# One-tile expert units from the ninth last routing batch on, and expert weights laid out by partition

## The chip, the cores and the metric

The kernel runs on one core of a Trainium2 chip. The metric is the device time of one execution in microseconds (us), the median of three. A core has TensorE (PE, matrix products; PEld is its weight load), VectorE (DVE), ScalarE (ACT), GpSimd (POOL) and SyncE (SP), each with its own queue of instructions, and 16 DMA engines that move data between DRAM and on-chip memory. Engines meet only at semaphores: an instruction that waits holds up everything behind it on its engine.

## The reference

A graph layer for 12,500 nodes of 256 features and 212,500 edges, followed by a mixture of 8 experts:

```python
xn = _layernorm(x)
x = x + gnn(xn, src, dst, edge_weight, ...) + mix(xn, ...)
h = _layernorm(x)
# experts: D = 256, F = 1024, E = 8, C = ceil(1.25 * 12500 / 8)
idx = argmax(softmax(h @ gate_w + gate_b)); prb = its probability
pos = running count of tokens of the same expert; kept = pos < C
y = (relu(h @ w1[idx] + b1[idx]) @ w2[idx] + b2[idx]) * prb * kept
x = x + nan_to_num(y)
```

`gnn` gathers `xn[src]` for each edge, weights it and sums it by `dst`. All data are 32-bit floats.

## The kernel before

**Pairs.** The edges are cut into 416 groups of 512, taken two at a time: 208 pairs. The program of every engine runs over "places" `p`. In each place below `PAIRS` (208) POOL gathers the rows of a pair (8 indirect DMAs, L776, into a ring of three pairs), DVE builds the one-hot matrices, PE multiplies (L855) and turns the sums (L865), DVE adds them to `acc` (L1283).

**Tokens.** From place `FIRST_C` (57) on a tile `t` of 128 tokens enters as soon as its edges are summed (`enters`) and passes nine steps in the following places (`c_step`): mixing, graph output, normalisation, the gate's logits. The last of 98 tiles enters in place 207. Tiles are routed in 20 batches (`routes`): first of seven tiles, then of four, the last of three. Routing finds each token's expert and position and a table that lists, for each slot of 128 tokens, which tokens are in it. A batch is known at `slots_at`; the last at place 219 (`last_c`).

**Expert units.** A unit is a pair of slots of one expert, 256 tokens. `units_after(b)` is how many units are sure to be full after batch `b`, whatever the routing; the last batch brings all the rest. There are K = 56 units, 112 slots. A unit has five ticks. In tick 0 PE transposes its rows (L1014), in ticks 1 to 4 it does two of the eight 128-wide chunks of the first layer each (L1024); the second layer of a tick (L1043) follows one tick later. ACT copies the transposed rows (L1742), applies relu (L1751) and scales the result (L1758). DVE adds the bias (L1517) and cleans the result (L1523 to L1528) during the next unit.

**Planner.** Ticks are laid into places by a budget of PE time (`PE_PLACE`, `PE_EXPERT`, `PE_STEP`), at most two in one place up to `last_c` and one in each after it. From the tick places follow those of the loads by SP (`load_first` L649, L651 and `load_second` L658, L660, one expert's weights for each unit, two buffers), of the row gathers by POOL (`gather_unit` L792) and of the results: units that are done before place 207 are kept by SP in DRAM (`keep_unit` L665), loaded back four at a time (`load_back` L676) and added to `out` by POOL later, in quiet places (`scatter_back` L813); the others are added by POOL directly (`scatter_unit` L802). A result buffer (`yo`, three of them) is free once its unit is kept or added.

**Order on an engine.** In a place, POOL does: gather of the first group, unit gathers, gather of the second, scatters, back-scatters. PE does: the pair's products, then `early` (small routing products), unit ticks, `late` (token steps).

Of the kernel before, what the change touches and what calls it, by code (L numbers as in the profile page):

```python
# [29 lines left out]
def build(nc, x, src, dst, weight, dst_grouped, gnn_w1t, gnn_b1, gnn_w2t, gnn_b2,  # L30
          wqt_bq, wkv, bkv, v_gamma, v_beta, k_scale, mix_w1, mix_b1, mix_w2, mix_b2,
          gate_w, gate_b, ffn_w1, ffn_b1, ffn_w2, ffn_b2, out, edges):
# [7 lines left out]
    FF = ffn_w1.shape[2]  # L40
# [9 lines left out]
    EXPERT_UNITS = SLOT_TILES // UNIT_TILES  # L50
    K = (N + NE * (UNIT - 1)) // UNIT
    SLOTS = K * UNIT_TILES
    TICKS = 1 + FC // 2
# [7 lines left out]
    assert GJ * GROUP * P <= LAP and UNIT_TILES * H * P <= 512 and FC % 2 == 0  # L61
# [6 lines left out]
    with ctx:  # L68
# [19 lines left out]
        kept_d = nc.dram_tensor("kept_scratch", [-(-K // BACK_UNITS), P, BACK_ROWS * D], F32).ap()  # L88
# [151 lines left out]
        def early_row(c):  # L240
# [3 lines left out]
        w1_sb = [behind(0, H, FF) for _ in range(2)]  # L244
        w2_sb = [behind(0, FC, D) for _ in range(2)]
        b1_sb = [behind(0, FC) for _ in range(2)]
# [14 lines left out]
        (col_i, col_odd, col_tile, col_from, full_at, some_at, count, full, fresh, ranked, queue_at, queue_base) = (  # L261
            behind(1, 1) for _ in range(12))
# [154 lines left out]
        def units_after(b):  # L417
# [6 lines left out]
        batch_of = [next(b for b in range(len(routes)) if k < units_after(b)) for k in range(K)]  # L424

        def small_steps(p):
# [10 lines left out]
            for b in range(len(routes)):  # L437
                if slots_at[b] == p and units_after(b) > units_after(b - 1):
                    found.append(("slots", b))
# [11 lines left out]
        e_ticks = [(k, j) for k in range(K) for j in range(TICKS)] + [(K, j) for j in range(TICKS)]  # L451
# [31 lines left out]
        def place_of(k, j):  # L483
            return e_place[k * TICKS + j]


        w1_at, w2_at, gather_at, scatter_at = ([[] for _ in range(PLACES)] for _ in range(4))
        for k in range(K):
# [5 lines left out]
            lag = 3 if place_of(k + 1, TICKS - 1) < PAIRS - 3 else 1  # L494
            scatter_at[min(place_of(k + 1, TICKS - 1) + lag, PLACES - 1)].append(k)

        KEEP_BEFORE = PAIRS - 1
        kept = [k for p in range(KEEP_BEFORE) for k in scatter_at[p]]
        assert kept == list(range(len(kept)))
        keep_at = [scatter_at[p] if p < KEEP_BEFORE else [] for p in range(PLACES)]  # L500
        scatter_at = [[] if p < KEEP_BEFORE else scatter_at[p] for p in range(PLACES)]
# [15 lines left out]
        def y_value(k):  # L517
            return 16 * UNIT_TILES * sum(i >= len(kept) for i in range(k % YS, k + 1, YS))
# [37 lines left out]
        assert SLOT_AT + 3 * UNIT_TILES * max(units_after(b) - units_after(b - 1) for b in range(len(routes))) <= 2 * P  # L556

        def relu_value(k, j):
            return 2 * ((TICKS - 1) * k + j)

        def l1_value(k, j):
            return (TICKS - 1) * k + j


        def sync_program(sp):
# [75 lines left out]
            def expert_of(k):  # L641
                sp.wait_ge(q_ready, sum(units_after(b) > units_after(b - 1) for b in range(batch_of[k] + 1)))
                return sp.value_load(expert_i[:, UNIT_TILES * k:UNIT_TILES * k + 1], min_val=0, max_val=NE - 1)

            def load_first(k):
                x_ = expert_of(k)
                if k >= 2:
                    sp.wait_ge(l1_relu, relu_value(k - 2, TICKS - 1))
                sp.dma_start(w1_sb[k % 2], ffn_w1[bass.ds(x_, 1)].rearrange("a (h p) f -> p (a h) f", p=P)  # L649
                             ).then_inc(w1_ld[k % 2], 16)  # L650
# [1206 lines left out]
```

## Time and profile before

| | |
|---|---|
| Median of three runs | 2673.07 us (2669.90 to 2673.34) |
| Profiled execution | 2668.34 us, its span 2666.6 us |
| PE busy | 2188.9 us (82%) |
| POOL busy | 1921.0 us (72%) |
| DVE busy | 1468.1 us (55%) |
| ACT busy | 995.7 us (37%) |
| DRAM read, written | 444.96 MB, 74.40 MB |
| Mean granted TensorE clock | 0.94 |

Times in rows are microseconds from the start of the span. "Idle before" is the time for which the engine stood before the instruction, and what it waited for; "issue" means that it waited for nothing that the profile shows. PE records two matmuls for each product of 32-bit floats in the program, so L1024 and L1043 have 32 records each per two-tile unit. The clock is the share of full speed: 1.00 is 2.4 GHz and 0.50 is 1.2 GHz.

### The profile page before, as it was taken

The numbers are of one execution on the slowest core, as the hardware profiler recorded it, in microseconds if no ns is written. First come the engines' busy times: TensorE is split into PE (matmuls) and PEld (weight loads), VectorE is DVE, ScalarE is ACT, GpSimd is POOL, SyncE is SP. The second block draws the span as 40 slices with busy tenths as digits, with TensorE's granted clock in tenths as the row PEclk, the third lists the DMA queues.
The fourth block names the chain that finished last, engine by engine and source line by source line (L and its number), as shares of the span: only waits on it lengthen the run. The fifth ranks groups of instructions, "written<-read, shape, count | busy, mean of one in ns | idle before, by whom it ended". The sixth has DMA issues, their size and how long they took to land. (4 is left out here: it accounts for less than half of the span.)

```text
span 2666.6 us, 40750 instructions
## 1 busy us (share of the span) xinstructions
PE 2188.9 (82%) x12096; PEld 1675.1 (63%) x12096; DVE 1468.1 (55%) x4510; ACT 995.7 (37%) x2211; POOL 1921.0 (72%) x1905
## 2 busy tenths in 40 slices
PE   0079999995667887989989988889889998879997
PEld 0036555553455655777767766777777776768886
DVE  5855544444357776777646545655554555552222
ACT  4623222220244444554433433433334334323332
POOL 7267777777777777777777777777777777457772
PEclk9999999997799998999999999998999898979999
DMA  9655555554466667666677666666656666669973
GB/s 331 227 164 166 163 160 160 160 163 122 141 183 179 180 175 238 193 208 198 211 217 229 213 211 211 199 207 211 217 188 204 209 190 214 187 179 248 234 201 89
DMA packets 347352, 518.45 MB, mean 194 GB/s; under 512 B 59554, under 2 KB 266258, under 8 KB 346004
## 3 DMA queue, kind: packets, MB, share of 16 engines
q0 software_dynamic: 101376, 243.85, 33.3%
q1 hardware_dynamic: 215366, 233.56, 27.7%
q10 hardware_dynamic: 30390, 38.41, 4.0%
q8 instruction: 101, 1.65, 0.3%
q14 instruction: 119, 0.97, 0.1%
HBM read 444.96 MB, written 74.40 MB: 195 GB/s over the span
## 5 line engine op out<-in xcount | busy, mean ns | idle before, releaser
L776 POOL DMA_INDIRECT rows_sb<-xn_scratch,src_sb x1600 | 1564.5, 978 | 539.5 <-issue 533.7
L855 PE MATMUL bank<-rows_sb,s_sb 128*48 128x256 f32 x3200 | 436.0, 419 | 240.7 <-DMA rows_sb<-xn_scratch,src_sb 238.6
L855 PEld LDWEIGHTS bank<-rows_sb,s_sb 128*48 128x48 f32 x3200 | 224.8, 133 | 381.9 <-issue 267.0
L1043 PE MATMUL bank<-acc 128*128 128x256 f32 x1792 | 433.3, 386 | 9.5 <-DVE acc L1517 9.5
L1024 PE MATMUL bank<-acc 128*128 128x256 f32 x1792 | 433.3, 388 | 0.0
L1043 PEld LDWEIGHTS bank<-acc 128*128 128x128 f32 x1792 | 342.9, 194 | 56.9 <-issue 9.1
L1024 PEld LDWEIGHTS bank<-acc 128*128 128x128 f32 x1792 | 341.4, 195 | 44.2
L1283 DVE TENSOR_TENSOR acc<-acc,bank 128x96 f32 x416 | 106.1, 255 | 439.2 <-PE bank L865 193.1
L1751 ACT ACTIVATE acc<-bank,acc 128x256 f32<-128x256 f32 x448 | 188.0, 471 | 405.1 <-PE bank L1024 405.0
L1677 ACT COPY sums<-bank 112x256 f32<-112x256 f32 x208 | 76.8, 369 | 556.8 <-PE bank L855 556.7
L1708 ACT ACT_TABLE_LOAD x95 | 121.9, 1283 | 173.8 <-PE bank L946 172.9
L886 PE MATMUL bank<-arena 128*128 128x512 f32 x392 | 185.6, 596 | 0.0
L802 POOL DMA_INDIRECT out_dram<-acc,sca_i x48 | 75.2, 1566 | 101.7 <-DVE acc L1528 89.1
L792 POOL DMA_INDIRECT acc<-h_scratch,gat_i x112 | 110.7, 988 | 43.0 <-issue 30.5
L931 PE MATMUL bank<-arena,weff 128*128 128x128 f32 (+1 forms) x784 | 114.4, 292 | 28.8 <-ACT arena L1732 28.8
L931 PEld LDWEIGHTS bank<-arena,weff 128*128 128x128 f32 x784 | 106.9, 204 | 44.2 <-issue 41.0
L813 POOL DMA_INDIRECT out_dram<-rows_sb,sca_i x64 | 103.2, 1612 | 34.7 <-issue 18.6
L1267 DVE TENSOR_TENSOR s_sb<-s_sb,wgt_sb 128x384 f32<-128x384 f32 x208 | 116.8, 562 | 7.1
L1692 ACT ACTIVATE arena<-bank 128x512 f32<-128x512 f32 x98 | 58.5, 597 | 159.2 <-PE bank L886 159.2
L1361 DVE TENSOR_TENSOR arena<-bank,bias_sb 128x256 f32<-128x256 f32 x98 | 41.2, 420 | 135.1 <-PE bank L946 134.8
L1265 DVE TENSOR_TENSOR s_sb<-rel_sb,iota_win 128x384 f32<-128x384 f32 x208 | 113.7, 546 | 3.0 <-PE bank L855 1.6
L942 PE MATMUL bank<-w2m_sb,arena 128*128 128x256 f32 x392 | 107.8, 400 | 4.3 <-DVE arena L1366 4.3
(221 smaller groups left out, 3388.8 us busy)
## 6 DMA issues: line engine op xcount, KB each, us to landing
acc<-ffn_w_in SPq DMA_DIRECT2D x112, 1024.0 KB, 6.2
rows_sb<-xn_scratch,src_sb POOLq DMA_INDIRECT x1600
arena<-xn_scratch SPq DMA_DIRECT2D x194, 128.0 KB, 3.0
xnt_scratch<-arena SPq DMA_DIRECT2D x97, 128.0 KB
arena<-xnt_scratch SPq DMA_DIRECT2D x97, 128.0 KB
arena<-x_in SPq DMA_DIRECT2D x97, 128.0 KB
h_scratch<-arena ACTq DMA_DIRECT2D x97, 128.0 KB
out_dram<-arena ACTq DMA_DIRECT2D x97, 128.0 KB
```

Source lines behind the costliest of these rows:

```text
L776: pool.indirect_dma_start(out=rows_sb[:, c % ROW_SLOTS, :], out_offset=None, in_=xn_d, in_offset=bass.IndirectOffsetOnAxis(ap=src_sb[:, c: ...
L792: pool.indirect_dma_start(out=xs[:, k % 2 * UNIT_TILES + i, :], out_offset=None, in_=h2_d[0:tokens, :], in_offset=bass.IndirectOffsetOnAxi ...
L855: m = pe.matmul(psum[0][i * HALF:i * HALF + WIN, 0:D], s_sb[:, p % S_SLOTS, i * GROUP + j, :], early_row(c) if p < EARLY_PAIRS else rows_s ...
L886: m = pe.matmul(kv[0:r, :], xnt[:, t % R1, h, 0:r], wkv_sb[:, h, :], start=False, stop=h == H - 1)
L931: m = pe.matmul(psum[2][:, f * P:f * P + r], weff[:, h, f * P:(f + 1) * P], c_xnt[:, t % XS, h, 0:r], start=h == 0, stop=h == H - 1)
L942: pe.matmul(mix, c_hid[:, par, f, 0:r], w2m_sb[:, f, :], start=f == 0, stop=f == H - 1)
L1024: m = pe.matmul(bank[:, i * UNIT:(i + 1) * UNIT], w1_sb[k % 2][:, h, f * P:(f + 1) * P], xt[:, k % 2, h, :], start=h == 0, stop=h == H - 1)
L1043: m = pe.matmul(bank[:, i * D:(i + 1) * D], hid[:, f, i * P:(i + 1) * P], w2_sb[k % 2][:, f, :], start=f == 0 and i == 0, stop=f == FC - 1 ...
L1265: link(dve.tensor_tensor(s, rel_sb[:, c0:c0 + c].unsqueeze(2).broadcast_to(wide), iota_win[:, :].unsqueeze(1).broadcast_to(wide), ALU.is_e ...
L1267: dve.tensor_tensor(s, s, wgt_sb[:, c0:c0 + c].unsqueeze(2).broadcast_to(wide), ALU.mult).then_inc(s_built, 1)
L1708: act.activation(c_hid[:, par, f, 0:r], psum[2][:, f * P:f * P + r], ACT.Gelu, bias=beff[:, f:f + 1]).then_inc(c_gelu, 1)
L1751: act.activation(hid[:, f, :], bank[:, i * UNIT:(i + 1) * UNIT], ACT.Relu, bias=b1_sb[k % 2][:, f:f + 1]).then_inc(l1_relu, 1)
```

## The change

From the ninth last batch on (`SINGLE_FROM`) a unit is one slot of 128 tokens. There are then 105 slots in 82 units: 23 of two tiles and 59 of one. A one-tile unit has three ticks: the transposes, and two with four chunks of the first layer each. Cleaning a result is tied to the tick at which its unit ended (`last_tick`, `FLUSH`) instead of to the next unit's ticks. Only two-tile units are kept and loaded back (23; before 32). The quiet places of the back-scatters are chosen anew: up to two in one place, and one unit in each unit after the last token. The first-layer weights and its bias are one array, laid out so that a partition reads one run of 8,224 bytes; the second-layer weights likewise, 8,192 bytes. Before, a partition read two runs of 4,096 bytes and one of 32, and eight runs of 1,024.

```diff
-    K = (N + NE * (UNIT - 1)) // UNIT
-    SLOTS = K * UNIT_TILES
+    SLOTS = (N + NE * (P - 1)) // P
+    SINGLE_BATCHES = 9
+    FLUSH = 5
...
+        def tiles_after(b):
             if b < 0:
                 return 0
             if b == len(routes) - 1:
-                return K
-            return max(0, ((routes[b][-1] + 1) * P - NE * (UNIT - 1)) // UNIT)
+                return SLOTS
+            tokens = (routes[b][-1] + 1) * P
+            if b < SINGLE_FROM:
+                return UNIT_TILES * max(0, (tokens - NE * (UNIT - 1)) // UNIT)
+            return max(0, (tokens - NE * (P - 1)) // P)
+        units = []
+        for b in range(len(routes)):
+            size = UNIT_TILES if b < SINGLE_FROM else 1
+            units += [(b, at, size) for at in range(tiles_after(b - 1), tiles_after(b), size)]
...
+        def per_tick(k):
+            return 2 * UNIT_TILES // size(k)
+        def ticks(k):
+            return 1 + FC // per_tick(k) if k < K else FLUSH
+        def done_place(k):
+            return e_place[last_tick[k] + FLUSH]
...
-        kept = [k for p in range(KEEP_BEFORE) for k in scatter_at[p]]
+        kept = [k for p in range(PAIRS - 1) for k in scatter_at[p] if size(k) == UNIT_TILES]
...
-        quiet = [p for p in range(PAIRS + 2, last_c + 4) if not gather_at[p]]
-        for k in range(K):
-            if place_of(k, 0) > last_c + 4:
-                quiet += [place_of(k, 1), place_of(k, 3)][:1 + k % 2]
+        quiet = [p for p in range(PAIRS + 2, last_c + 4) if not gather_at[p] for _ in range(1 + (p > PAIRS + 3))]
+        quiet += [place_of(k, 1) for k in range(K) if place_of(k, 0) > last_c + 4]
...
-                sp.dma_start(w1_sb[k % 2], ffn_w1[bass.ds(x_, 1)].rearrange("a (h p) f -> p (a h) f", p=P)
-                             ).then_inc(w1_ld[k % 2], 16)
-                sp.dma_start(b1_sb[k % 2], ffn_b1[:, bass.ds(x_, 1), :].rearrange("p a c -> p (a c)")
+                sp.dma_start(first_sb[k % 2], ffn_first[bass.ds(x_, 1)].rearrange("a p f -> p (a f)")
                              ).then_inc(w1_ld[k % 2], 16)
...
-                sp.dma_start(w2_sb[k % 2], ffn_w2[bass.ds(x_, 1)].rearrange("a (c p) d -> p (a c) d", p=P)
+                sp.dma_start(flat2(w2_sb[k % 2]), ffn_w2[bass.ds(x_, 1)].rearrange("a p f -> p (a f)")
...
-                        for i in range(2):
-                            f = 2 * (j - 1) + i
+                        for i in range(per_tick(k)):
+                            f = per_tick(k) * (j - 1) + i
                             for h in range(H):
-                                m = pe.matmul(bank[:, i * UNIT:(i + 1) * UNIT], w1_sb[k % 2][:, h, f * P:(f + 1) * P],
-                                              xt[:, k % 2, h, :], start=h == 0, stop=h == H - 1)
+                                m = pe.matmul(bank[:, i * tokens:(i + 1) * tokens], w1_sb[k % 2][:, h, f * P:(f + 1) * P],
+                                              xt[:, k % 2, h, 0:tokens], start=h == 0, stop=h == H - 1)
...
+    def rows_by_partition(v):
+        return v.reshape(v.shape[0], -1, P, v.shape[2]).transpose(0, 2, 1, 3).reshape(v.shape[0], P, -1)
```

## Rows read from the trace of the kernel before

**Rows 1.** The page: busy time, share of the span and instructions of each engine.
```profile
PE 2188.9 (82%) x12096; PEld 1675.1 (63%) x12096; DVE 1468.1 (55%) x4510; ACT 995.7 (37%) x2211; POOL 1921.0 (72%) x1905
```

**Rows 2.** Stretches: busy time by engine, clock, DMA share, GB/s.
```profile
139.70:2283.00 2143.30, 1845.19 (x10458) 1375.26 (x10459) 1240.85 (x3777) 793.39 (x1771) 1634.22 (x1671) 0.94 0.63 190
2400.00:2500.00 100.00, 100.00 (x479) 88.06 (x478) 26.68 (x43) 33.14 (x77) 75.75 (x53) 1.00 0.97 240
```

**Rows 3.** Line L776 (row gathers): duration min/median/max in ns, idle before by cause.
```profile
L776 POOL DMA_INDIRECT rows_sb<-xn_scratch,src_sb x1600: 949/953/1452, 139.7 to 2280.8; - x178
...
  issue: 533.7, 1581
```

**Rows 4.** Waits of POOL from 1000 to 2270 us: total, times, longest.
```profile
POOL rows_sb L776 <- issue: 276.8, 908, 0.3
...
POOL rows_sb L776 <- PE bank L855: 3.7, 12, 0.3
```

**Rows 5.** Stretches of 5 us between the stages, and one step of the timeline.
```profile
2295.00:2300.00 5.00, 1.84 (x15) 1.42 (x13) 1.44 (x6) 3.49 (x6) 3.33 (x3) 1.00 0.91 286
2300.00:2305.00 5.00, 0.94 (x5) 0.97 (x6) 2.46 (x10) 0.00 (x0) 3.69 (x4) 0.55 0.65 142
...
2365.00:2370.00 5.00, 0.84 (x5) 0.74 (x4) 3.45 (x19) 0.00 (x0) 3.78 (x5) 0.50 1.03 287
...
2304.06 1.09 PE L1014 MATMUL bank<-ident,acc 128*128 128x128 f32 x4 [4.98 <-DMA acc<-h_scratch,gat_i]
```

**Rows 6.** Timeline of a unit in the last stage: start, length, instruction.
```profile
2563.53 0.60 PE L1014 MATMUL bank<-ident,acc 128*128 128x128 f32 x4
...
2570.87 1.89 PE L1024 MATMUL bank<-acc 128*128 128x256 f32 x8
...
2572.80 0.84 ACT L1751 ACTIVATE acc<-bank,acc 128x256 f32<-128x256 f32 x2 [1.82 <-PE bank L1024]
...
2577.78 0.60 PE L1014 MATMUL bank<-ident,acc 128*128 128x128 f32 x4
```

**Rows 7.** Timeline: eight records of 128 columns, then four of 256.
```profile
1906.69 1.05 PE L931 MATMUL bank<-arena,weff 128*128 128x128 f32 x8
...
1907.59 1.03 PE L942 MATMUL bank<-w2m_sb,arena 128*128 128x256 f32 x4
```

**Rows 8.** Line L802 (scatters): duration, and issue to landing.
```profile
L802 POOL DMA_INDIRECT out_dram<-acc,sca_i x48: 1552/1554/1684, 2282.1 to 2658.5; - x48
...
DMA to landing us min/median/max: 2.7/5.4/8.5
```

**Rows 9.** Stretches for the DMA rates: last two numbers are share and GB/s.
```profile
10.00:20.00 10.00, 0.00 (x0) 0.00 (x0) 8.81 (x38) 3.92 (x9) 7.67 (x8) 1.00 1.02 395
20.00:30.00 10.00, 0.00 (x0) 0.00 (x0) 3.79 (x18) 6.56 (x12) 7.62 (x8) 1.00 1.02 409
2270.00:2275.00 5.00, 5.00 (x33) 3.88 (x30) 3.33 (x10) 0.37 (x1) 3.78 (x5) 1.00 0.33 98
2325.00:2330.00 5.00, 5.00 (x27) 3.96 (x26) 0.48 (x2) 1.31 (x5) 4.09 (x4) 1.00 0.64 77
...
2315.00:2320.00 5.00, 5.00 (x24) 4.38 (x24) 2.24 (x5) 2.69 (x8) 0.00 (x0) 1.00 0.99 407
2370.00:2375.00 5.00, 2.45 (x10) 2.31 (x11) 3.59 (x18) 0.32 (x1) 4.09 (x4) 0.50 1.11 351
...
2618.40:2632.70 14.30, 14.30 (x70) 12.60 (x69) 3.76 (x6) 4.74 (x11) 3.29 (x3) 1.00 0.51 157
2504.40:2518.70 14.30, 14.30 (x70) 12.60 (x69) 3.75 (x6) 4.74 (x11) 8.35 (x7) 1.00 1.05 279
```

**Rows 10.** Timeline: SP's long issues, and the end after the last product.
```profile
2425.21 2.81 SPq L660 DMA_DIRECT2D acc<-ffn_b_in  x1
...
2651.03 0.69 DVE L1517 TENSOR_TENSOR acc<-bank,acc 128x512 f32<-128x512 f32 x1 [5.54 <-PE bank L1043]
...
2658.52 1.55 POOL L802 DMA_INDIRECT out_dram<-acc,sca_i  x1 [0.30 <-issue]
```

More of the change, by code:

```diff
@@ L243, in build @@
         YS = 3
-        w1_sb = [behind(0, H, FF) for _ in range(2)]
+        first_sb = [behind(0, H * FF + FC) for _ in range(2)]
+        w1_sb = [v[:, 0:H * FF].rearrange("p (h f) -> p h f", h=H) for v in first_sb]
+        b1_sb = [v[:, H * FF:] for v in first_sb]
         w2_sb = [behind(0, FC, D) for _ in range(2)]
-        b1_sb = [behind(0, FC) for _ in range(2)]
         b2_sb = [behind(1, D) for _ in range(2)]
@@ L260, in build @@
         sprb = behind(1, SLOTS)
-        (col_i, col_odd, col_tile, col_from, full_at, some_at, count, full, fresh, ranked, queue_at, queue_base) = (
-            behind(1, 1) for _ in range(12))
+        (col_i, col_odd, col_tile, col_from, full_at, one_at, some_at, count, full, fresh, ranked, queue_at, queue_base) = (
+            behind(1, 1) for _ in range(13))
         ld_gmin, ld_edges, ld_gbc = sem("ld_gmin"), sem("ld_edges"), sem("ld_gbc")
@@ L420, in units_after, with size, columns_of, gathered @@
             if b == len(routes) - 1:
-                return K
-            return max(0, ((routes[b][-1] + 1) * P - NE * (UNIT - 1)) // UNIT)
-        batch_of = [next(b for b in range(len(routes)) if k < units_after(b)) for k in range(K)]
+                return SLOTS
[7 more added lines that the diff above has]
+            units += [(b, at, size) for at in range(tiles_after(b - 1), tiles_after(b), size)]
+        K = len(units)
+        batch_of = [b for b, _, _ in units]
+        def size(k):
+            return units[k][2]
+        def columns_of(k):
+            return range(units[k][1], units[k][1] + size(k))
+        def per_tick(k):
+            return 2 * UNIT_TILES // size(k)
+        def ticks(k):
+            return 1 + FC // per_tick(k) if k < K else FLUSH
+        def gathered(k):
+            return 16 * sum(size(i) for i in range(k % 2, k + 1, 2))
+        queued = [b for b in range(len(routes)) if tiles_after(b) > tiles_after(b - 1)]
+        def queue_value(b):
+            return sum(i <= b for i in queued)
         def small_steps(p):
@@ L437, in small_steps @@
             for b in range(len(routes)):
-                if slots_at[b] == p and units_after(b) > units_after(b - 1):
+                if slots_at[b] == p and b in queued:
                     found.append(("slots", b))
@@ L450, in build @@
         PE_STEP = {1: 1.2, 3: 3.0, 7: 0.5, 8: 0.7}
-        e_ticks = [(k, j) for k in range(K) for j in range(TICKS)] + [(K, j) for j in range(TICKS)]
+        e_ticks = [(k, j) for k in range(K + 1) for j in range(ticks(k))]
+        first_tick = [n for n, (k, j) in enumerate(e_ticks) if j == 0]
+        last_tick = [first_tick[k] + ticks(k) - 1 for k in range(K)]
         e_place, time, p = [], 0.0, FIRST_C
@@ L517, in y_value @@
         def y_value(k):
-            return 16 * UNIT_TILES * sum(i >= len(kept) for i in range(k % YS, k + 1, YS))
+            return 16 * sum(size(i) for i in range(k % YS, k + 1, YS) if i >= len(kept))
         def kept_value(k):
@@ L784, in gather_unit @@
                 if k == 0 or batch_of[k - 1] != b:
-                    pool.wait_ge(q_ready, sum(units_after(i) > units_after(i - 1) for i in range(b + 1)))
+                    pool.wait_ge(q_ready, queue_value(b))
                     for t in range(max(0, routes[b][-1] + 1 - OS), routes[b][-1] + 1):
@@ L1038, in unit_tick @@
                         pe.wait_ge(y_biased, y_bank_before(k) + 1)
-                for f in (2 * j - 2, 2 * j - 1):
-                    tiles = range(UNIT_TILES)
+                for f in range(per_tick(k) * (j - 1), per_tick(k) * j):
+                    tiles = range(size(k))
                     for i in tiles if f < FC - 1 else reversed(tiles):
@@ L1501, in unit_tick @@
             def unit_tick(n):
[L1502 to L1513 removed]
+                for k in range(K):
+                    step = n - last_tick[k]
+                    if not 2 <= step <= FLUSH:
+                        continue
+                    y = yo[:, k % YS * UNIT_TILES:k % YS * UNIT_TILES + size(k), :]
+                    mask, clip = mask_sb[:, 0:size(k), :].bitcast(I32), clip_sb[:, 0:size(k), :]
+                    if step == 2:
+                        product = psum[y_bank(k)][:, 0:size(k) * D].rearrange("p (i d) -> p i d", d=D)
+                        dve.wait_ge(w2_ld[k % 2], 32 * (k // 2 + 1))
+                        dve.wait_ge(l2_mm, l1_done(k))
+                        if k >= YS and k - YS < len(kept):
```

141 lines of the change are left out of this document (65 added, 76 removed).

## The prediction

> **What bounds the kernel now.** I read the page's busy shares first [rows 1]: PE 82%, POOL 72%, neither full, so the bound changes by stage. Next the stretches by engine [rows 2]. Up to about 2283 us (208 pairs of edge groups, with the token work beside them) PE is below full; from about 2400 us (expert units alone) it is busy for the whole of each stretch. What holds the first stage is seen in the gather line of POOL [rows 3]: 1600 gathers of 0.95 us, and nearly all the idle time before them is "issue", 0.30 us each; POOL's own waits in 1000 to 2270 us show no other engine worth naming [rows 4]. Each gather therefore costs POOL 1.25 us, back to back: 1600 + 70 of them fill 139.7 to 2283 us at 1.28 us. So the pair stage is POOL's, and PE's waits for rows are its shadow. Between 2283 and about 2390 us neither is full: PE idles in two stretches and its clock drops to 1.2 GHz (0.50) [rows 5]. One idle piece is 4.98 us for the gather of a unit known only just before; the next is the routing of the last tokens, where no unit is left. From there a unit of two tiles takes 14.25 us of PE from transpose to transpose, at 2.4 GHz, with no gap [rows 6]: less 0.43 for four transposes (at the 0.11 of [rows 7]) that is 0.216 for each of 64 matmul records.
>
> **Where the units lie.** Running the planner's formulas (FIRST_C 57, PAIRS 208, last_c 219) for both versions gives first-layer tiles per span of places: up to 170, 46 and 46; 171 to 207, 24 and 21; 208 to 219, 6 and 8; from 220, 36 and 30. Sum 112 and 105. The slots fall from 112 to 105 since a half-empty unit now wastes at most 127 tokens of an expert, not 255.
>
> **PE per tile: no change.** The new first layer has 32 records of 128 columns for each tile instead of 32 of 256 for two. The form is in the trace: eight records of 128 columns with changing weights take 1.05 us, the last ending 0.28 after its start, so 0.11 each; four of 256 take 1.03 [rows 7]. A one-tile unit then is 2 x 0.108 + 32 x 0.108 + 16 x 0.216 = 7.12 us, half of 14.25. No gain and no loss per tile. The eight relus (at 0.42 us for 256 columns in [rows 6], less for 128) and six DVE steps on half the columns stay below 7.1 us.
>
> **Pair stage: +31 us.** Units of two tiles whose scatter falls before place 207 are kept by SP and added later. The new one-tile units are not kept: 18 of them (23 to 40) have their scatter place before 207, so POOL issues it there. A scatter costs POOL 1.55 + 0.30 = 1.86 us [rows 8]; two unit gathers fewer (68 against 70). 18 x 1.86 - 2 x 1.25 = +31.0 us on the engine that sets this stage, between +28 and +34 (issue gaps as they are, or one in two hidden). Their other side, 9 kept units and 18 back-scatters fewer later, frees POOL where it does not bind. SP issues 21 instead of 12 unit loads there; transfers that PE needs are asked for a place (10.5 us) early, and the row ring holds three pairs, so I cost the extra traffic (about 50 GB/s) at nothing; uncovered it would be PE waits, which reach POOL only after two places. A new wait can bite: DVE's bias of unit k waits for the scatter of k-3, and in 8 cases both are in the same place. DVE would stand some 5 us (landing 5.4 [rows 8]); behind it is the one-hot of the next pair, and behind that PE, which has two places before POOL waits. Taken as 0, bounds 0 to +15.
>
> **Places 208 to 219: -10 us.** Unit work in 208 to 212 falls from ten ticks of 2.85 to ten of 2.37 (-4.8). The 4.98 us wait for a fresh gather goes, since the units there are from batches routed long ago (-5). Places 213 to 216, empty before, get 19 us of units while DVE does its 5 to 8 us of routing per place: mostly covered, +4 for ticks that stand ahead of a routing product in PE's order; and PE, busier, should not fall to 1.2 GHz, where it spent some 10 us of work at double price [rows 5] (-4). No row shows this arrangement: bounds -20 and +8.
>
> **From place 220, PE alone: -42.8 us.** 36 x 7.125 = 256.5 becomes 30 x 7.125 = 213.8, if everything arrives.
>
> **From place 220, transfers: +19 us.** This is the term that decides. Each unit, of one tile or two, loads 2.23 MB of weights and biases; per 14.25 us before, per 7.12 after. DMA is already at share 1.05 in a full unit [rows 9]. What must fit into 7.12 us: weights and biases; the new layout gives 8 KB runs. Near it are the first 30 us of the kernel (7 KB runs beside gathers: 395, 409 GB/s) and the stretch with the 8 KB runs of the kept rows (407): 5.5 us at 405. Upper end is the last unit's load in old layout, share 0.51 over 14.3 us = 7.3. Gather 0.33 (its bytes at 400 GB/s) to 0.42 (share 0.33 in 5 us, four gathers). Scatter-add: at least 0.33; the stretch with little else but back-scatters has share 0.64 for 2.6 of them, 1.2 each; it both reads and writes the target, so I take 0.85, the middle. A unit without back-scatter: 5.5 + 0.35 + 0.85 = 6.7, below 7.12, PE stays the bound. With one (units 55 to 68, 14 of them, two more scatter-adds each): 8.4, 1.3 over, 18 us; two back loads (1.84 MB) 4.6; less about 4 us by which loads run ahead: +19. Lower bound 0 (scatters at 0.33). Upper +87 (1.2 and 7.3: 11.3 and 8.9 us). POOL needs 1.28 + 1.86 + 2 x 1.9 = 7.0 us in such a unit, just under PE.
> The Trainium skill speaks against the change here. Rows first: 395 to 409 GB/s. "DMA: Bandwidth & Descriptors", section "Where 436 GB/s comes from", says that between HBM and SBUF about 358 GB/s binds; weights at that rate would take 6.2 us, an estimate from the page, and the tail some 15 us more. The rows exceed it, so the sum goes by them.
>
> **The end: -4 us.** From the last bias step, which follows PE's last matmul, to the end of the span 15.6 us now [rows 10]: bias, scaling, five DVE steps on 512 columns (0.69 to 0.43) and two scatters. On 256 columns about 2.2 less, and one scatter (1.86) less.
>
> **Sum.** Against the profiled execution (2668.34 us, span 2666.6): +31.0 - 10 - 42.8 + 19 - 4 = -6.8, so 2661.5. That execution lies 4.7 below the median of 2673.07; in terms of the median, 2666.3, taken as 2666.
>
> **Rivals.**
> 1. Transfers keep up (scatter-adds at 0.33 to 0.45): the +19 goes, 2647. For it: PE lost nothing at share 1.05; against it: SP's issue of a load, 0.4 us as a rule, already lasts 2.81 us where much is queued [rows 10].
> 2. Slower: the transfers bind the whole tail. Weights at 6.4 us (the 351 GB/s of a saturated stretch with share 1.11 [rows 9]) and scatter-adds at 1.2: 10.4 us with back-scatter, 8.0 without, 14 x 3.3 + 16 x 0.9 + 4.6 - 4 = 61, that is 2708. It decides from about 8.9 us per unit with back-scatter, where the gain is used up.
> 3. The 18 scatters cost POOL nothing visible: 2635. Rows 3 and 4 speak against it.
> 4. The waits on the three result buffers, with the middle stretch as long as now: +10 and +10, 2686.
> 5. The loads never move faster than the 351 GB/s that a saturated stretch shows [rows 9], so weights take 6.4 us, with scatter-adds as forecast: 9.3 with back-scatter, 7.6 without, 14 x 0.9 + 16 x 0.5 = 21 on the forecast, 2687. The 395 to 409 of the same group speak against it. (The Trainium skill's 358 in "DMA: Bandwidth & Descriptors" would come out near here.)
>
> **How the numbers follow.** Forecast 0.42, its own range 2652 to 2682; rival 1 0.22; rival 2 0.17; rival 3 0.04; rival 4 0.08; rival 5 0.07. Range 2642 to 2700: it leaves out rival 3, the far part of rival 2 and a little of 1. A measurement of this kernel tells about 0.2% (5.3 us) from no change. Faster: rivals 1 and 3 and half of the forecast, 0.47. Same: a third of the forecast, a part of 5 and 4, 0.20. Slower 0.33.
>
> **What would show it.** Last row gather near 2312 us, not 2281; POOL without idle before it but "issue"; PE periods of 7.12 us in the last 13 units, and about 8.4 while back-scatters run, with waits of PE on weight or row transfers there; no PE clock of 0.50 in the routing of the last tokens; the same 0.11 us per 128-column record. Wrong it would be if PE waits for transfers throughout the tail, if the last row gather comes earlier than 2300, or if the middle stretch gets longer.

## The result and the profile after

The changed kernel takes 2693.14 us (median of four runs, 2689.43 to 2701.53); the kernel before 2673.16 in the same comparison. The ratio is 1.0079, 95% interval 1.0064 to 1.0094: 20 us slower, where 7 us less was forecast. The execution that was profiled for after is the slowest of the four (2701.53 us, span 2699.8), and that of before is faster than all four of its runs (2668.34), so the two traces stand 33 us apart, not 20. Four of the experiments land below both kernels; the best takes 2643 us.

The page of after, busy time of each engine, beside [rows 1]:

```profile
PE 2174.9 (81%) x12802; PEld 1679.2 (62%) x12802; DVE 1483.1 (55%) x4668; ACT 1018.5 (38%) x2438; POOL 1911.8 (71%) x1891
```

PE is busy 14 us less. The two layers of the units take 35 us less (866.6 in L1043 and L1024 before, 831.9 in L1076 and L1057 after; seven slots fewer), and the products of the pairs, x3200 in both, take 20 us more (456.1 against 436.0). The kernel is longer all the same, so the answer lies in what each stage waits for. I cut the span at two marks that both traces have: the start of the last row gather (where the pair stage hands over) and the transposes of the first unit of place 220. Stretches of before, then of after, cut there (columns: length, busy time of PE, PEld, DVE, ACT, POOL, granted clock, DMA share, GB/s):

```profile
2280.80:2392.50 111.70, 86.89 (x423) 74.38 (x420) 59.03 (x217) 35.58 (x79) 51.07 (x36) 0.83 0.72 187
2392.50:2666.60 274.10, 258.43 (x1233) 227.29 (x1231) 71.76 (x115) 86.13 (x200) 170.17 (x119) 0.98 0.77 195
```

```profile
2321.10:2455.80 134.70, 101.66 (x592) 90.68 (x593) 61.75 (x235) 42.33 (x124) 50.98 (x36) 0.83 0.74 223
2455.80:2699.80 244.00, 224.18 (x1508) 207.92 (x1508) 75.66 (x186) 92.16 (x301) 125.63 (x90) 0.97 0.94 312
```

| stage | before | after | difference | forecast |
|---|---|---|---|---|
| to the last row gather | 2280.8 | 2321.1 | +40.3 | +31 |
| from there to place 220 | 111.7 | 134.7 | +23.0 | -10 |
| from place 220 to the end | 274.1 | 244.0 | -30.1 | -27.8 (-42.8 + 19 - 4) |

The first and the last term came out within 10 us of the forecast. The middle one has the wrong sign, and it alone makes 33 of the 40 us between the forecast (6.8 us less) and the trace (33.2 more).

**Pair stage.** Row gathers and token scatters of after, as [rows 3, 8] (durations min/median/max in ns, first and last start), and POOL's waits from 1800 to 2316 us:

```profile
L811 POOL DMA_INDIRECT rows_sb<-xn_scratch,src_sb x1600: 942/954/1523, 139.7 to 2321.1; - x178
```

```profile
L835 POOL DMA_INDIRECT out_dram<-acc,sca_i x59: 1552/1571/1914, 1967.9 to 2691.8; - x59
```

```profile
POOL rows_sb L811 <- issue: 105.2, 345, 0.3
...
POOL out_dram L835 <- issue: 5.5, 18, 0.3
```

As foreseen: 18 scatters stand in POOL's order with gaps of 0.3 us of issue, and POOL's waits for other engines in that window come to 2.1 us in all. Between 1945 and 2325 us the scatters take 30.0 us busy, 1.67 on average and not 1.55, plus 0.30 each: 35.4. The two unit gathers fewer give 2.5 back. The rest of the 40.3 is in the row gathers themselves, of which the pages of before and after say:

```profile
L776 POOL DMA_INDIRECT rows_sb<-xn_scratch,src_sb x1600 | 1564.5, 978 | 539.5 <-issue 533.7
```

```profile
L811 POOL DMA_INDIRECT rows_sb<-xn_scratch,src_sb x1600 | 1572.2, 983 | 539.5 <-issue 533.4
```

They take 7.7 us more, 5 ns each: 35.4 - 2.5 + 7.7 = 40.6. In the other kernels with the new layout this total is 1567.5 to 1571.2, in after with the old layout 1565.8. That the layout does it is likely, but with one profiled execution of each it is not shown.

**The middle.** PE is busy 14.8 us longer there (the stage holds two tiles more, of about 7.1 us each) and idle 8.2 longer (24.8 before, 33.0 after). But its waits are not the same waits. Sums of PE's waits by cause, in us (the first wait of after starts 1.3 us ahead of the mark, that of the last column 2.7):

| PE waits for | before | after | after, kept rows first (below) |
|---|---|---|---|
| DVE's steps of routing and tokens | 15.9 | 1.4 | 3.5 |
| the rows of a unit (gather) | 6.7 | 12.2 | 0 |
| the rows of the last pair | 0 | 8.1 | 7.9 |
| second-layer weights | 0 | 9.8 | 10.5 |
| other | 2.2 | 2.4 | 4.2 |

So the units moved here did fill the time in which PE used to wait for routing, of which two waits of before are

```profile
2364.42 0.59 PE L979 MATMUL bank<-arena,upper 128*128 128x24 f32 x2 [5.16 <-DVE arena L1551]
...
2370.84 0.59 PE L985 MATMUL bank<-acc,upper 128*128 128x1 f32 x2 [5.00 <-DVEq L1464]
```

and three other waits came in their place. The first is for the rows of the last pair. In before PE reaches that pair at 2289.12, 8.3 us behind the last gather, and is busy until then; in after it has nothing left to do from 2319.76 on:

```profile
2327.82 3.66 PE L887 MATMUL bank<-rows_sb,s_sb 128*48 128x256 f32 x16 [8.06 <-DMA rows_sb<-xn_scratch,src_sb]
```

(16 such records take 1.93 us in before; the clock is 0.50 from 2325 to 2335.) The longest wait is for a unit's gather, as POOL and then PE show it (start, length, instruction, idle before and its cause):

```profile
2351.40 1.59 POOL L835 DMA_INDIRECT out_dram<-acc,sca_i  x1 [13.78 <-DVE acc L1562]
2371.59 1.56 POOL L845 DMA_INDIRECT out_dram<-rows_sb,sca_i  x1 [18.60 <-DMA rows_sb<-kept_scratch]
...
2375.32 1.02 POOL L826 DMA_INDIRECT acc<-h_scratch,gat_i  x1 [0.30 <-issue]
```

```profile
2382.26 0.66 PE L1046 MATMUL bank<-ident,acc 128*128 128x128 f32 x2 [12.20 <-DMA acc<-h_scratch,gat_i]
```

POOL stands 18.60 us at the first back-scatter, for kept rows that SP asked for only at 2359.31; behind it in POOL's order is the row gather of a unit (L826), and PE waits 12.20 us for that. Before had nearly the same stall, with no harm, since the gathers were issued ahead of it (trace of before):

```profile
2303.66 0.95 POOL L792 DMA_INDIRECT acc<-h_scratch,gat_i  x1 [0.30 <-issue]
2320.08 1.62 POOL L813 DMA_INDIRECT out_dram<-rows_sb,sca_i  x1 [15.47 <-DMA rows_sb<-kept_scratch]
```

Two more waits are for second-layer weights (L1076), each with the clock at half behind it: 3.75 us for eight records that take 1.89 otherwise. The profile names the load for the first alone; the second ends at 2451.60, when the load of the same kind that SP issued at 2441.76 had landed (2451.51).

```profile
2415.68 1.89 PE L1076 MATMUL bank<-acc 128*128 128x256 f32 x8
2426.75 3.75 PE L1076 MATMUL bank<-acc 128*128 128x256 f32 x8 [4.94 <-DMA acc<-ffn_b_in]
...
2451.60 3.75 PE L1076 MATMUL bank<-acc 128*128 128x256 f32 x8 [4.89 <-issue]
```

Both loads are issued late in SP's order, with no wait of their own shown. The one for the first wait goes out at 2416.35, right behind a load of first-layer weights that stands until 2415.09 for ACT to release its buffer (L686, the second of two that the row merges); the one for the second wait goes out at 2441.24, behind such a load that stands until 2439.98.

```profile
2404.66 10.92 SPq L686 DMA_DIRECT2D acc<-ffn_first_in  x2
2416.35 0.33 SPq L693 DMA_DIRECT2D acc<-ffn_w_in  x1
```

**From place 220.** A unit in the last part of after, and stretches of 50 us, which answer to [rows 6, 9]:

```profile
2620.64 0.38 PE L1046 MATMUL bank<-ident,acc 128*128 128x128 f32 x2
...
2622.59 3.73 PE L1057 MATMUL bank<-acc 128*128 128x128 f32 x32
...
2627.89 0.38 PE L1046 MATMUL bank<-ident,acc 128*128 128x128 f32 x2
```

```profile
2450.00:2500.00 50.00, 46.27 (x295) 41.57 (x296) 13.16 (x32) 16.63 (x55) 35.24 (x25) 0.94 1.06 336
2500.00:2550.00 50.00, 45.30 (x293) 42.22 (x293) 14.51 (x36) 17.36 (x58) 31.50 (x22) 0.93 1.03 338
2550.00:2600.00 50.00, 48.59 (x331) 44.83 (x330) 15.78 (x39) 21.38 (x70) 32.09 (x23) 1.00 1.06 361
2600.00:2650.00 50.00, 50.00 (x348) 46.87 (x347) 16.59 (x41) 21.02 (x69) 17.66 (x14) 1.00 0.99 335
```

A unit takes 7.25 us, not 7.12: its 32 records of 128 columns take 3.57 us from first to next (2622.59 to 2626.16), 0.112 each. 29 periods of 7.25 and 21.2 us behind the last transposes make 231.4; the stage took 244.0, so 12.6 us were lost to transfers and queues, where I had put 19. Of these 7.8 are idle time of PE (19.8 in the stage, less 12.0 behind its last product), and 4.8 are products that took longer, as those at half clock behind a wait do.

### The profile page after: what moved, and what is told of

Same layout as the page of the kernel before. It is cut to its first block and busy times, and to the rows that moved or that the text cites. A ratio compares the mean times of both kernels' runs of the same rounds, so it can differ in the third digit from the quotient of the medians.

```text
span 2699.8 us, 42881 instructions
## 1 busy us (share of the span) xinstructions
PE 2174.9 (81%) x12802; PEld 1679.2 (62%) x12802; DVE 1483.1 (55%) x4668; ACT 1018.5 (38%) x2438; POOL 1911.8 (71%) x1891
## 5 line engine op out<-in xcount | busy, mean ns | idle before, releaser
L811 POOL DMA_INDIRECT rows_sb<-xn_scratch,src_sb x1600 | 1572.2, 983 | 539.5 <-issue 533.4
L887 PE MATMUL bank<-rows_sb,s_sb 128*48 128x256 f32 x3200 | 456.1, 434 | 275.0 <-DMA rows_sb<-xn_scratch,src_sb 274.9
L887 PEld LDWEIGHTS bank<-rows_sb,s_sb 128*48 128x48 f32 x3200 | 235.4, 137 | 424.0 <-issue 335.8
L1076 PE MATMUL bank<-acc 128*128 128x256 f32 x1680 | 412.7, 390 | 25.9 <-DVE acc L1551 10.5
L1057 PE MATMUL bank<-acc 128*128 128x128 f32 (+1 forms) x2624 | 419.2, 315 | 5.0 <-issue 5.0
L1057 PEld LDWEIGHTS bank<-acc 128*128 128x128 f32 x2624 | 374.2, 201 | 25.9 <-issue 6.1
L1076 PEld LDWEIGHTS bank<-acc 128*128 128x128 f32 x1680 | 318.6, 197 | 68.0 <-issue 25.9
L1786 ACT ACTIVATE acc<-bank,acc 128x128 f32<-128x128 f32 (+1 forms) x656 | 212.1, 397 | 387.1 <-PE bank L1057 383.9
L835 POOL DMA_INDIRECT out_dram<-acc,sca_i x59 | 94.5, 1601 | 110.1 <-DVE acc L1562 95.6
L826 POOL DMA_INDIRECT acc<-h_scratch,gat_i x105 | 104.9, 999 | 79.5 <-PE bank L1046 53.9
L1557 DVE TENSOR_TENSOR acc<-acc 128x256 int32<-128x256 f32 (+1 forms) x82 | 41.1, 501 | 176.1 <-ACT acc L1793 171.1
```

The lines of the kernel that those rows point to most:

```text
L811: pool.indirect_dma_start(out=rows_sb[:, c % ROW_SLOTS, :], out_offset=None, in_=xn_d, in_offset=bass.IndirectOffsetOnAxis(ap=src_sb[:, c: ...
L887: m = pe.matmul(psum[0][i * HALF:i * HALF + WIN, 0:D], s_sb[:, p % S_SLOTS, i * GROUP + j, :], early_row(c) if p < EARLY_PAIRS else rows_s ...
L1057: m = pe.matmul(bank[:, i * tokens:(i + 1) * tokens], w1_sb[k % 2][:, h, f * P:(f + 1) * P], xt[:, k % 2, h, 0:tokens], start=h == 0, stop ...
L1076: m = pe.matmul(bank[:, i * D:(i + 1) * D], hid[:, f, i * P:(i + 1) * P], w2_sb[k % 2][:, f, :], start=f == 0 and i == 0, stop=f == FC - 1 ...
L1786: act.activation(hid[:, f, 0:tokens], bank[:, i * tokens:(i + 1) * tokens], ACT.Relu, bias=b1_sb[k % 2][:, f:f + 1]).then_inc(l1_relu, 1)
```

## The experiments

My theory after reading this: the pair stage pays for scatters that are no longer kept, and the middle for the order of POOL and SP around the kept rows. The rivals: a change in the loads' rate or layout, and PE work that has grown by itself. Four kernels ran first on a chip on which the kernel before took 3158.64 us. Another bound held the pair stage there: with the new layout alone, POOL stood 249 us for what the profile calls "remote" and 216 us for PE. The ratios to before on that chip were 1.0139 (1.0078 to 1.0200) for after with the back-scatters later, 0.9988 (0.9953 to 1.0024) for three single batches and 1.0133 (1.0077 to 1.0189) for after with the old layout. These three are not used; they ran again elsewhere, with everything that follows (single executions of before there: 2668 to 2682 us). All stretches in the table below are of the one profiled execution of each kernel, in us. Kernels that are the same up to the last row gather (those with three single batches) differ there by up to 3.9 us, so differences of that size between single stretches say nothing.

| kernel | median | ratio to before (95%) | last row gather | middle | from place 220 |
|---|---|---|---|---|---|
| before | 2673.16 | 1 | 2280.8 | 111.7 | 274.1 |
| after | 2693.14 | 1.0079 (1.0064 to 1.0094) | 2321.1 | 134.7 | 244.0 |
| three single batches | 2657.34 | 0.9941 (0.9924 to 0.9958) | 2283.7 | 135.6 | 240.0 |
| after, back-scatters later | 2687.72 | 1.0053 (1.0035 to 1.0072) | 2321.5 | 116.6 | 249.4 |
| after, all units kept | 2676.74 | 1.0014 (1.0004 to 1.0023) | 2283.0 | 137.0 | 257.8 |
| three, back-scatters later | 2649.22 | 0.9917 (0.9900 to 0.9933) | 2285.1 | 125.0 | 237.1 |
| three, loads later | 2650.05 | 0.9911 (0.9895 to 0.9928) | 2287.3 | 134.7 | 227.0 |
| three, both edits | 2643.15 | 0.9872 (0.9847 to 0.9896) | 2287.6 | 128.6 | 226.1 |
| after, kept rows first | 2690.88 | 1.0056 (1.0036 to 1.0077) | 2320.8 | 120.0 | 244.6 |
| after, old layout | 2695.31 | 1.0089 (1.0072 to 1.0106) | 2313.9 | 130.1 | 248.9 |

**The layout alone.** The kernel before with the new arrays and nothing else; one of its lines:

```diff
...
-                sp.dma_start(w2_sb[k % 2], ffn_w2[bass.ds(x_, 1)].rearrange("a (c p) d -> p (a c) d", p=P)
+                sp.dma_start(flat2(w2_sb[k % 2]), ffn_w2[bass.ds(x_, 1)].rearrange("a p f -> p (a f)")
...
```

> The kernel before with the new weight layout alone (runs of 8,224 and 8,192 bytes, one DMA for first layer and bias), units of two tiles as before. PE waits for no weight load in the tail before, so theory A expects 2673 within 4 us, with a smaller DMA share in a full unit (0.85 instead of 1.05). Rival: the layout helps the middle stretch by itself, 2660 to 2668.

Measured: 1.0005 (0.9976 to 1.0033), on the chip just named. No difference that can be told there. The DMA share in full units fell, but by less than expected: in a unit of the tail without back-scatters it is 0.47 (3112.4 to 3126.6) against 0.51 before at the same 157 GB/s, so 6.7 us for a load and not 7.3; in most others it is 0.71 to 0.96.

**The new units with the old layout** (the same lines the other way round, in after).

> The changed kernel with the old weight layout, on a chip where the kernel before takes about 2673 us (the first attempt ran where it took 3159 and was no slower there than the run with later back-scatters). My prediction's price of short runs (7.3 us per load of a unit, not 5.5) would make units from place 220 on take 8 to 9 us: 2718 to 2743. If run length matters little, within 5 us of 2693.

Measured: 2695.31 us against 2693.14, no difference to speak of; the 25 us or more that my price of short runs gives are excluded. Its stretches, beside those of after above:

```profile
2450.00:2500.00 50.00, 44.47 (x290) 40.49 (x289) 14.52 (x36) 17.15 (x56) 29.21 (x21) 0.97 1.07 333
...
2600.00:2650.00 50.00, 50.00 (x347) 46.92 (x346) 16.76 (x41) 20.91 (x70) 18.09 (x14) 1.00 1.03 330
```

The same bytes arrive at 330 to 339 GB/s with share 1.03 to 1.10, against 335 to 361 with 0.99 to 1.06: runs of 1,024 bytes cost the DMA engines a few per cent, and PE, full from 2600 on in both, does not see it. In the single traces the stages differ by more than the medians: from place 220 on the old layout takes 4.9 us longer, the pair stage 7.2 us less (6.4 of them row gathers), the middle 4.6 less. The near-equality of the totals may thus be a sum of a gain and a loss.

**Only the last three batches in one-tile units.** No scatter of a one-tile unit then falls before place 207 (by the planner's formulas), 32 units are kept as before, and the units of place 220 and after hold 27 tiles, not 30.

```diff
-    SINGLE_BATCHES = 9
+    SINGLE_BATCHES = 3
```

> One-tile units from the third last batch on, once more, on another chip: on the first chip of the experiments the kernel before itself took 3159 us, since POOL waited there for rows (470 us beyond its issue gaps), so that 18 scatters on POOL could hide. Where POOL is back to back (kernel before near 2673), theory A/C still expects the last row gather near 2281 and 2630 to 2650 us in all; rival B 2660 to 2680.

Measured: 2657.34 us, 35.8 below after and 15.8 below before. The last row gather starts at 2283.7, 37.4 us earlier than in after. That is the price of the 18 scatters (less two gathers), and it fits the 35.4 - 2.5 read from the trace plus the 4.7 us by which the row gathers are shorter here (1567.5 against 1572.2). The gain is less than I expected (2630 to 2650 us): although PE has three tiles fewer from place 220 on (21.8 us), that stage is only 4.0 us shorter than in after. The middle is as long as in after, with the same wait:

```profile
2334.34 1.62 POOL L845 DMA_INDIRECT out_dram<-rows_sb,sca_i  x1 [29.28 <-DMA rows_sb<-kept_scratch]
```

```profile
2345.04 0.66 PE L1046 MATMUL bank<-ident,acc 128*128 128x128 f32 x2 [12.15 <-DMA acc<-h_scratch,gat_i]
```

**After with the back-scatters later**, from place 216 on, two in a place, so that none stands ahead of that gather.

```diff
-        quiet = [p for p in range(PAIRS + 2, last_c + 4) if not gather_at[p] for _ in range(1 + (p > PAIRS + 3))]
+        quiet = [p for p in range(PAIRS + 8, last_c + 4) if not gather_at[p] for _ in range(2)]
```

> Back-scatters from place 216 on, once more, on another chip. Theory A: PE's 12.2 us wait before the transposes of the one-tile unit in place 211 is gone and the whole is 10 to 18 us faster than the changed kernel (about 2680). Rival B: no gain, up to 9 us slower.

Measured: 2687.72 us, 5.4 below after and not 10 to 18; the intervals of the two ratios overlap. The 12 us wait is gone and the middle falls from 134.7 to 116.6, so the wait did come from POOL's order; but 5.4 us come back from place 220 on, where more back-scatters now lie, and the two waits for second-layer weights stay (4.48 and 4.60).

**After with all early units kept**, one-tile ones too: they are written to DRAM by SP and added later, so the 18 scatters leave the pair stage while the units stay as they are.

```diff
-        kept = [k for p in range(PAIRS - 1) for k in scatter_at[p] if size(k) == UNIT_TILES]
+        kept = [k for p in range(PAIRS - 1) for k in scatter_at[p]]
...
```

Two things in the order of work change with it: SP keeps results ahead of its unit loads in a place, not behind them, and units after 68 get two places for back-scatters.

> The changed kernel (one-tile units from the ninth last batch on) with its 18 one-tile units that are done before place 207 kept by SP and added later, like the two-tile ones; SP keeps ahead of its loads in a place. This removes the 18 scatters from POOL's pair stage and leaves the middle stretch and the tail's periods alone. Theory A/C (POOL pays them in full): last row gather at 2284 to 2288 us, not 2321, and the whole 2655 to 2668, with up to 10 us of the 37 given back where 18 more scatter-adds run in the last 13 units. Rival (the shift is absorbed later, since the middle stretch waits on something else): the whole stays at 2680 or above.

Measured: the last row gather at 2283.0, 38 us earlier; the kernel only 16.4 faster than after, at 2676.74: neither the 2655 to 2668 of the theory nor the 2680 or more of the rival. From place 220 on it takes 257.8 us, 13.8 more than after, with PE gaps of 3.79, 4.30 and 4.68 us, and SP stands 26.4 us in three waits for back-scatters. So the scatters' 38 us can be taken off POOL there, but 18 more back-scatters and their kept rows cost a good part of it in the tail. Three single batches beat this kernel from place 220 on (240.0 against 257.8), where they have 27 tiles and not 30; up to the last row gather the two are alike (2283.7 and 2283.0).

**Three batches with the back-scatters later** (from place 213, two in a place):

```diff
-        quiet = [p for p in range(PAIRS + 2, last_c + 4) if not gather_at[p] for _ in range(1 + (p > PAIRS + 3))]
+        quiet = [p for p in range(PAIRS + 5, last_c + 4) if not gather_at[p] for _ in range(2)]
```

> One-tile units from the third last batch on (2657 us) with back-scatters from place 213, two in each free place, not from 210. Theory A (a unit gather stands on POOL behind a back-scatter that waits for kept rows): PE's wait of 12.2 us before the transposes near 2345 us goes, and the whole is 5 to 12 us faster, 2645 to 2652. Rival: the wait moves to the second-layer weights (5.5 and 4.9 us now) and the gain is under 3 us.

Measured: 2649.22, 8.1 us below the three batches alone, as expected; the middle 125.0 instead of 135.6. The waits for second-layer weights (5.41, 5.70) and three gaps in the tail (4.51, 5.18, 7.26) stay.

**Three batches with kept rows asked for later.** In the tail, SP asks for the next group of kept rows one place after the back-scatter that frees its buffer, and stands until that has landed; the loads of the next unit are behind it. In the trace of three single batches (SP's queue, then PE):

```profile
2500.39 0.33 SPq L711 DMA_DIRECT2D rows_sb<-kept_scratch  x1
2501.52 0.33 SPq L686 DMA_DIRECT2D acc<-ffn_first_in  x1
```

```profile
2510.42 6.02 PE L1057 MATMUL bank<-acc 128*128 128x128 f32 x32 [6.62 <-issue]
```

```profile
SPq L710 <- DMA out_dram<-rows_sb,sca_i: 26.9, 3, 9.3
```

```diff
-            back_ld_at[PAIRS + 1 if i < BACK_SLOTS else back_place[backs[i - BACK_SLOTS][-1]] + 1].append(i)
+            back_ld_at[PAIRS + 1 if i < BACK_SLOTS else back_place[backs[i - BACK_SLOTS][-1]] + 4].append(i)
```

> One-tile units from the third last batch on with the later loads of kept rows three places later in SP's order. In the run before, SP stood 26.9 us in three waits for back-scatters to land, and PE then lost 4.7, 6.6 and 6.2 us before first-layer products and ran them at 1.2 GHz (6 us, not 3.7). Theory D (SP's order, not the rate of transfers, makes these gaps): all three go and the whole is 15 to 25 us faster, 2633 to 2643. Rival B (the DMA engines are full, share 1.02): the gaps come back elsewhere, gain under 5 us.

Measured: 2650.05, 7.3 us below, less than expected. SP's wait falls from 26.9 to 9.0 us, the three gaps of 4.7 to 6.6 us are gone (one of 2.9 is left before a first layer) and the tail is 13.0 us shorter in the profiled execution, but units of 10 to 12 us remain (2510 to 2521 and 2543 to 2555) while the DMA share is 1.07; I take them for the megabytes of kept rows, whose transfer has to be fitted in somewhere. The 12 us wait in the middle (12.64) is untouched, as it should be.

**Both edits on three batches.**

> Three single batches, with both edits: back-scatters from place 213 on, two in a place, and kept rows of the fourth and later groups asked for four places after their buffer is given up. If the two losses are separate (POOL in order behind kept rows in the middle, SP in order behind a back-scatter's landing in the last stage), the gains add: 2657.3 - 8.1 - 7.3 = about 2642. If the load of kept rows only moves and takes its DMA time wherever it falls, no more than the better of the two edits: 2649. In both cases the 12 us PE wait for a fresh gather is gone, and the SP wait for a back-scatter stays below 10 us in all. The two waits of about 5 us for second-layer weights stay by either, since neither edit touches them.

Measured: 2643.15 us (2638.39 to 2647.75), 14.2 below the three batches alone where the two edits by themselves gave 8.1 and 7.3: they add within the noise, so these are two losses, one in POOL's order and one in SP's. SP's wait came to 11.1 us in four, a little over the 10 that I had set. It is the fastest kernel of this study, 1.3% below before. Still there is the wait for second-layer weights:

```profile
2387.47 3.75 PE L1076 MATMUL bank<-acc 128*128 128x256 f32 x8 [5.07 <-DMA acc<-ffn_b_in]
```

**After with kept rows first in SP's order of a place.**

```diff
+                for i in back_ld_at[p]:
+                    load_back(i)
                 for k in w1_at[p]:
                     load_first(k)
                 for k in w2_at[p]:
                     load_second(k)
...
-                for i in back_ld_at[p]:
-                    load_back(i)
```

> The kernel after with one change: within a place SP asks for kept rows ahead of the unit loads, not behind them. My theory: the 18.6 us for which POOL stood at a back-scatter, and with it the 12.2 us of PE for the gather behind it, come from SP's order (kept rows asked for at 2359 instead of 2310 us). Then the first three groups of kept rows are issued some 40 us earlier, the 12.2 us wait is gone or below 3 us, and the time is 8 to 12 us less than that of the kernel after: about 2682. Rival: SP's order is not what counts, since kept rows, 1 MB each, three at a time, only take the rate from the unit weights, which then come later: the 12.2 us go, but PE waits for weights by as much, 2690 to 2695. Second rival: SP already stands at these loads for another reason (all pairs must be through PE first), and the kept rows are issued at 2340 or later in either order: no change.

Measured: the kept rows are asked for at 2338.48 instead of 2359.31, 21 us earlier and not 40. SP stands until 2332.15 at an earlier load of second-layer weights, whose buffer DVE has to release, and the last pair's products, for which the load of kept rows waits in any order, end only at 2329.66. The stall and the 12 us wait are gone:

```profile
2349.15 1.67 POOL L845 DMA_INDIRECT out_dram<-rows_sb,sca_i  x1 [0.30 <-issue]
2351.12 1.55 POOL L845 DMA_INDIRECT out_dram<-rows_sb,sca_i  x1 [0.30 <-issue]
2352.98 1.02 POOL L826 DMA_INDIRECT acc<-h_scratch,gat_i  x1 [0.30 <-issue]
```

and the middle takes 120.0 us instead of 134.7. The medians are 2.3 us apart and the ratios to before 0.0023 (6 us), with intervals that overlap: the mechanism is shown by the trace, the 8 to 12 us that I expected of it are not. The waits for weights (4.70 and 5.77) are still there, and a third, of 7.17 us before a second layer at 2491.67, is in the last stage. Since the profiled execution of after is 8.4 us above its median and this one 3.8 below its own, part of the 14.7 us between the traces is chance.

## Why the prediction was wrong

**Pair stage, +31: right in kind, too small.** 18 scatters at 1.97 us instead of 1.86, and row gathers that take up to 7.7 us more in all, for which the sum had no term; 37 to 40 in all. Moving them out (two kernels) gives 37.4 and 38.1 back, so POOL did set this stage and rival 3 is dead. The cost that I took as nothing, DVE waiting for a landed scatter, is 3.3 us in one wait between 1945 and 2325, and POOL's waits show nothing of it.

**Places 208 to 219, -10: the step that failed.** The stage got 23.0 us longer. The cover that I forecast did come: PE's waits for routing and token steps fell from 15.9 to 1.4 us. What failed is that the sum let one wait go (-5) and priced no new one.

First, the order of queues. I wrote that the 4.98 us wait for a gather would go, since the units there had been routed long ago. When a unit is known does not matter if its gather stands in POOL's order behind a back-scatter, which waits for kept rows, which SP asks for behind unit loads. I had the rows for this: kept rows first asked for at 2310, POOL standing 15.47 us for them. I had looked at which waits end, not at what would now be queued behind that wait. This is 12.2 us of PE in the trace; the four kernels in which the gather no longer stands behind a late back-scatter lose it. With kept rows first the middle is 14.7 us shorter, 6.3 of them busy time (the clock there is 0.90, not 0.83). What the wait is worth in the median is less: 2.3 and 5.4 (after) and 8.1 us (three batches), of which the 2.3 is no more than noise.

Secondly, PE met two waits that were nowhere in my sum: 9.8 us for second-layer weights, and 8.1 us for the rows of the last pair. They use up what the cover had won. Even with kept rows first the middle takes 120.0 us, 8.3 more than before: PE is busy 8.5 us more, and idle as long as before (24.7 against 24.8), for these causes in place of the routing. No run takes either wait away by itself, so what each is worth in the median is open. The wait for the last pair's rows is 6.0 to 8.1 us in all five kernels with nine single batches, while with three it is 3.8 in one and under 2.5 in the others.

**My statement that PE would no longer drop to 1.2 GHz** was wrong too. In the routing of the last tokens the clock is back at 1.00 most of the time, but it falls behind the new waits: 0.50 from 2325 to 2335, 0.50 to 0.58 in parts of 2425 to 2455, and in the stretch 2375 to 2380 with PE at rest. The mean over the stage is 0.83 as before.

```profile
2375.00:2380.00 5.00, 0.00 (x0) 0.00 (x0) 1.70 (x7) 0.00 (x0) 3.78 (x5) 0.50 1.04 357
```

**From place 220, PE alone, -42.8.** 30 tiles at 7.25 are 217.5, so -39.0 by the same sum: 0.112 us for each 128-column record in a run of 32, where I took 0.108.

**Transfers there, +19: near in size, by a working that the runs do not bear out.** The loss was 12.6 us. But the new layout is worth about 2 us in the median, not the gap between 5.5 and 7.3 us per load, and a unit with back-scatters needs less than my 8.4 us. The kernel with kept rows first has a stretch that shows it:

```profile
2500.00:2550.00 50.00, 50.00 (x346) 46.78 (x345) 16.68 (x41) 21.38 (x70) 39.82 (x28) 1.00 1.05 345
```

Seven units with 14 back-scatters, 7 scatters and 7 gathers (POOL's 28) go through with PE never idle, in 7.25 us each. The transfers do not quite keep that pace. In the five periods from 2510.00 to 2546.25 SP's queue moves 10.79 MB, where five units load 11.16, so the supply would give about 7.5 us per unit; and the back-scatters take 8.2 us to land at the start of the stretch and 10.6 at its end (medians of 2497 to 2513 and 2534 to 2552). The queue of POOL's indirect transfers takes, of 16 engines, in this stretch and in 2600 to 2650 of after, where 7 scatters and 7 gathers run:

```profile
q0 software_dynamic: 3029, 3.02, 32.6%
```

```profile
q0 software_dynamic: 1200, 1.14, 12.9%
```

The difference is 9.9 us for 14 back-scatters, 0.70 each: not far below the 0.85 that I took, and above rival 1's 0.33 to 0.45. What made 8.4 too much is not settled by these rows; part of it is that the shares add to more than 1.00 in full stretches (1.05 to 1.10), where I had taken 1.00 as full. The rest of what is lost in the tail is lost in gaps, four to seven us long, when a megabyte of kept rows and SP's wait for its buffer come between two units' loads; moving that load took three of them away. So rival 1 (transfers keep up) comes near in PE's pace, though not in its price, and rivals 2 and 5 (10.4 and 9.3 us per such unit) are refuted by the same rows. The Trainium skill's 358 GB/s ("DMA: Bandwidth & Descriptors", "Where 436 GB/s comes from") is near the fullest stretches of 50 us here (361; the kernel with both edits has 365), while single stretches of 5 us reach 434 (2370 to 2375 in after), so it is no fixed ceiling. Whether it or the work of the 16 engines sets the rate of the full stretches is not shown; where no back-scatters run, 335 GB/s are enough for a full PE.

**The end, -4**, came true: from the last bias step to the end of the span it is 11.9 us in after (2687.91 to 2699.8) against 15.6, so -3.7. It is contained in the 21.2 us behind the last transposes.

**The sum.** 40.3 + 23.0 - 30.1 = 33.2 between the traces. Against the medians it is 20; the same stages must be some 13 us shorter in a typical pair of executions, and which of them is not known, since only one execution is profiled. Rivals 4 and 5 (2686 and 2687) came nearest in time, each by a cause that the traces do not bear out: for rival 4 (waits on result buffers, the middle as long as before) DVE waited only 11.5 us for landed scatters in the whole kernel, in eight waits, and the middle got longer; rival 5's loads are answered above.

**Open.** The two waits of about 5 us for second-layer weights in the middle, with half-clock work behind, stay in every kernel with one-tile units; none of the edits touched their cause. In after both loads stand in SP's queue behind a load of first-layer weights that waits for its buffer; that asking for them in another order would end the waits was not tested. Nor was why PE runs out of work ahead of the last pair's rows, or whether the new layout makes the row gathers 5 ns longer.

## What to carry over

When a change moves small units of work earlier, list for each engine what stands behind every wait that is harmless today; a 15 us stall with nothing behind it became 12 us of PE when a gather was queued behind it. And when a wait is filled with work taken from elsewhere, ask where that work is now missing: here PE stood for the last pair's rows instead. On the engine that sets a stage, each instruction counts in full wherever its data come from, so cut work finer only where that engine has room: three batches instead of nine turned 0.8% slower into 0.6% faster, and two reorderings into 1.3%.

## What was not expected of the hardware

- Longer runs hardly help: 8 KB runs against runs of 4 KB (first layer) and 1 KB (second layer) of the same weights, 2 us in 2693, DMA share 0.99 against 1.03 at 335 and 330 GB/s.
- A gap costs more than its length: after waiting 4.7 us, PE's next 32 records of 128 columns took 6.37 us instead of 3.73, at half clock (after, 2509 us):

```profile
2509.14 6.37 PE L1057 MATMUL bank<-acc 128*128 128x128 f32 x32 [4.70 <-issue]
```

- An indirect scatter-add held POOL for 1.67 us on average in the pair stage (18 of them) and 1.57 in the later stages (41), and took 0.70 us of the 16 DMA engines' time.
